# Transposing the codes of x by DMA in place of TensorE in a fused quantized attention-and-LoRA kernel

## The reference

```python
def fake_quant(v, scale, zp):
    q = clip(round(v / scale + zp), 0, 255)
    return (q - zp) * scale

def xattn(x1, x2):                       # for each batch
    return fake_quant(x1, s1, z1) @ fake_quant(x2, s2, z2)

def ffn(x, A, B, Wr):                    # 4 experts of rank 16, top 2
    gates = softmax(keep_top2(x @ Wr.T))
    mid = einsum('tf,erf->ter', x, A)
    return sum_e(gates * einsum('ter,eor->teo', mid, B) * 4)

x = x + tanh(g_xattn) * xattn(layernorm(x), ctx)
x = x + tanh(g_ffn) * ffn(layernorm(x), A, B, Wr)
```

## Time and profile before

| | us |
|---|---|
| time, median of 3 runs | 429.81 (429.75 to 431.95) |
| the profiled execution's own time | 432.26 |
| its span in the profile | 430.5 |
| TensorE busy in the span | 360.3 (84%) |
| VectorE busy | 334.7 (78%) |
| ScalarE busy | 257.6 (60%) |
| GpSimd busy | 85.5 (20%) |
| mean granted clock of TensorE | 0.949 |

### The profile page before, as it was taken

How to read it: one execution, slowest core, us unless ns; L and a number is a source line. 1 busy time by engine, 2 the same in 40 slices (tenths; PEclk the granted TensorE clock), 3 DMA queues, 4 the chain that set the end, 5 groups by cost and what they waited for, 6 DMA issues and landing times. The chain is left out here.

```text
span 430.5 us, 7428 instructions
## 1 busy us (share of the span) xinstructions
PE 360.3 (84%) x2480; PEld 213.2 (50%) x2480; DVE 334.7 (78%) x764; ACT 257.6 (60%) x240; POOL 85.5 (20%) x74
## 2 busy tenths in 40 slices
PE   0063549679989998989899999999999999999954
PEld 0031224265555555555556464756565656565642
DVE  2549994897897979797979787879787878687584
ACT  1655698377859587776767455556464655555140
POOL 1000000130404030222222222222222222224020
PEclk9996779868999999999999999999999999999995
DMA  4999980246755645556472222222222222312022
GB/s 142 344 402 428 424 311 4 97 142 246 251 162 180 190 159 202 185 189 201 150 240 99 99 99 98 99 98 97 97 97 97 97 97 97 99 50 97 2 97 99
DMA packets 22241, 68.52 MB, mean 159 GB/s; under 512 B 3204, under 2 KB 3716, under 8 KB 20100
## 3 DMA queue, kind: packets, MB, share of 16 engines
q1 hardware_dynamic: 22216, 68.20, 44.4%
HBM read 51.42 MB, written 16.78 MB: 158 GB/s over the span
## 5 line engine op out<-in xcount | busy, mean ns | idle before, releaser
L539 PE MATMUL ps_main<-q,q1T 128*128 128x512 f16 x928 | 213.3, 381 | 0.0
L539 PEld LDWEIGHTS ps_main<-q,q1T 128*128 128x128 f16 x928 | 88.1, 99 | 101.9 <-issue 8.5
L404 ACT ACTIVATE h_hi<-x,small_tile 128x1024 f16<-128x1024 f32 x32 | 39.4, 1234 | 65.5 <-DVE small_tile L830 65.5
L349 POOL TENSOR_TENSOR h_lo<-work,h_hi 128x1024 f16<-128x1024 f32 x31 | 66.6, 2148 | 43.7 <-ACT work L409 41.9
L814 DVE SCALAR_TENSOR_TENSOR x<-ps_main,small_tile,xt 128x512 f32<-128x512 f32 x60 | 44.8, 747 | 23.8 <-DMA out_x<-x 14.5
L788 DVE BATCH_NORM_STATS2 small_tile<-xt 128x6 f32<-128x512 f32 x64 | 40.8, 683 | 16.8 <-DMA xt<-in_x 16.7
L343 POOL TENSOR_TENSOR small_tile<-small_tile 128x1 f32<-128x1 f32 x16 | 8.8, 549 | 210.3 <-DVE small_tile L826 210.3
L392 ACT ACTIVATE work<-xt,small_tile 128x1024 uint8<-128x1024 f32 x32 | 38.1, 1234 | 16.0 <-DVE small_tile L804 16.0
L819 DVE BATCH_NORM_STATS2 small_tile<-x 128x6 f32<-128x512 f32 x64 | 44.3, 692 | 1.7
L888 DVE TENSOR_TENSOR x<-ps_delta,x 128x512 f32<-128x512 f32 x64 | 42.3, 683 | 2.7 <-PE ps_delta L605 2.7
L382 ACT ACTIVATE ctx_stage<-ctx_stage,small_tile 128x1024 uint8<-128x1024 f32 x32 | 38.7, 1236 | 5.0 <-DMA ctx_stage<-in_ctx 5.0
(11 more groups left out here) (98 smaller groups left out, 401.9 us busy)
## 6 DMA issues: line engine op xcount, KB each, us to landing
xt<-in_x SPq DMA_DIRECT2D x32, 512.0 KB, 3.7
q<-in_ctx SPq DMA_DIRECT2D x16, 1024.0 KB, 17.8
ctx_stage<-in_ctx SPq DMA_DIRECT2D x32, 512.0 KB, 5.0
out_x<-x SPq DMA_DIRECT2D x64, 256.0 KB, 2.2
x<-in_L_ffn_A SPq DMA_DIRECT2D x1, 512.0 KB
x<-in_L_ffn_B SPq DMA_DIRECT2D x1, 512.0 KB, 15.9
small_tile<-in_L_xattn_x_scale SPq DMA_DIRECT2D x2, 0.5 KB, 4.2
small_tile<-in_L_xattn_x_zp SPq DMA_DIRECT2D x2, 0.5 KB, 4.7
```

Source lines behind the costliest of these rows:

```text
L349: nc.gpsimd.tensor_tensor(h_lo[:, h, :], work[:, h, :], h_hi[:, h, :], ALU.subtract).then_inc(h_lo_ready, 1)
L404: nc.scalar.activation(h_hi[:, h, :], x1[:, b % 2, half(h)], ACT.Identity, bias=h_bias[:, :], scale=h_rstd[:, :]).then_inc(h_hi_ready, 1)
L539: mm = pe.matmul(acc[:, :], q1T[:, b % 2, k, :], q2[:, batch(b), k, cols(n)], start=(k == 0), stop=(k == KT - 1))
```

## The change

From tile 2 on the codes of x are not transposed by TensorE. SP issues two transposing DMAs per tile (`dma_start_transpose`), one for each half of `q1_code`, straight into q1T. They wait for the rounding (x_rounded) and for the products of the tile that last used the buffer (main_done). `turn_q1` and `copy_q1T` are no longer called in the slots; tiles 0 and 1 keep them in the prologue. TensorE's products wait for the DMA's semaphores, and so does ScalarE before it writes `work` again. `turn_hi` waits for the copy of the low part (loT_ready) that last emptied its bank. On SP the two issues stand behind the context load of q = 0 (in slot 1 ahead of it).

```diff
+        q1T_loaded = [sem("q1T_loaded0"), sem("q1T_loaded1")]
...
+            def turn_q1(b, i, h):
+
+                wait(sp, x_rounded, b, i, 2, h + 1)
+                sp.sem_inc(sp_waited, 1)
+                wait(sp, main_done, b, i, NB, -NB)
+                sp.sem_inc(sp_waited, 1)
+                sp.dma_start_transpose(q1T[:, b % 2, h * HK:(h + 1) * HK, :], q1_code[:, h, :]).then_inc(q1T_loaded[h], 16)
+
...
+                if b == 1:
+                    turn_q1(b + 1, i, 0)
+                    turn_q1(b + 1, i, 1)
                 ctx_half(0)
+                if 2 <= b < TILES - 1:
+                    turn_q1(b + 1, i, 0)
+                    turn_q1(b + 1, i, 1)
...
             def normal_half(b, i, h):
-                wait(act, q1_turned, b, i, 2, h + 3)
+                if b == 0:
+                    act.wait_ge(q1_turned, h + 3)
+                else:
+                    wait(act, q1T_loaded[h], b, i, 16, 0)
...
-                    copy_q1T(b + 1, i, 0)
-                    copy_q1T(b + 1, i, 1)
...
-                if ahead:
-                    copy_q1T(b + 1, i, 0)
-                    copy_q1T(b + 1, i, 1)
...
             def turn_q1(b, i, h):
                 wait(pe, x_rounded, b, i, 2, h + 1)
-                wait(pe, loT_ready[h], b, i, 1, -1)
...
                     if n == 0 and k % HK == 0:
-                        wait(pe, q1T_ready, b, i, 2, k // HK + 1)
+                        wait(pe, q1T_loaded[k // HK], b, i, 16, -16)
...
             def turn_hi(b, i, h):
-                if b == TILES - 1:
-                    turn_h(b, i, h, h_hi, h_hi_ready, hi_turned, loT_ready[h], 1, 0)
-                    return
-
-                turn_h(b, i, h, h_hi, h_hi_ready, hi_turned, q1T_ready, 2, 3 + h)
+                turn_h(b, i, h, h_hi, h_hi_ready, hi_turned, loT_ready[h], 1, 0)
...
                         mid_lo(b - 1, i, h)
-                        if b < TILES - 1:
-                            turn_q1(b + 1, i, h)
                     main(b, i, 3, general)
```

More of the change, by code:

```diff
@@ L189, in build @@
         gated_ready, gate_turned, gT_step, gT_ready = sem("gated_ready"), sem("gate_turned"), sem("gT_step"), sem("gT_ready")
-        dve_waited = sem("dve_waited")
+        dve_waited, sp_waited = sem("dve_waited"), sem("sp_waited")
         delta_done, out_ready = sem("delta_done"), sem("out_ready")
@@ L256, in load_x @@
             def load_x(b, i, h):
+                rows = bass.ts(b, P) if isinstance(i, int) else bass.ts(i * 2 + b, P)
                 if b >= 2:
                     wait(sp, x1_ready, b, i, NB, 2 * h + 2 - 2 * NB)
-                rows = bass.ts(b, P) if isinstance(i, int) else bass.ts(i * 2 + b, P)
                 sp.dma_start(xt[:, b % 2, half(h)], x_rows[rows, half(h)]).then_inc(x_loaded[b % 2][h], 16)
@@ L286, in ctx_half @@
                     if b < PER_B - 1:
-                        wait(sp, ctx2_coded, b, i, Q, q + 1)
                         row = (HALVES + Q * (b + 1) + q) // 2
                         rows = bass.ts(row, P) if isinstance(i, int) else bass.ts(i * Q + row, P)
+                        wait(sp, ctx2_coded, b, i, Q, q + 1)
                         load_ctx(rows, q % 2, q)
```

## The result

The change makes no gain; it costs a little. The kernel before took 430.94 us (20 runs, 429.06 to 436.19), the changed one 433.68 us (20 runs, 430.71 to 437.2). The ratio is 1.0058 (95% interval 1.0035 to 1.0082). The prediction of 423.7 us was wrong by 10 us, though the time is inside its range. The profiled execution of after took 433.89 us, with a span of 432.2 us.

A forecast was written before the change was run, and what follows sets the result against it. TensorE's queue was taken to bound the kernel, with a second chain through x almost without slack in late tiles. Gains of 0.45 + 1.4 + 4.2 = 6.1 us off the 429.81 us median gave 423.7 us, range 418 to 441.

The forecast's parts named there:

- The ceiling: TensorE, tiles 2 to 15: sixteen transposes removed per tile, 0.90 us each tile, at most 12.6 us gained.
- the late regime: Slots 8 to 14, TensorE without gaps at 21.1 us per tile: 0.6 us gained per tile, 4.2 us (3.8 to 6.3).
- it fits: Late tiles: the gate's operand would be ready at 301.2, before TensorE reaches it at 301.3, so no new wait.
- The early regime: Slots 2 to 7, while second-batch context is coded: 0.24 us gained per tile, 1.4 us (0 to 4.2).
- The gate's wait of 0.4 us: Early tiles: sign of a right forecast, TensorE's wait for the gate's operand (L594 for L874) grows to 0.4 us.
- Slot 1: First changed slot: only the second eight transposes count, 0.45 us gained (0 to 0.9).
- L: Time from the end of the first rounding until both transposed halves land: taken as 6.9 us, free up to 9.0.
- the two bounds: Landing of one transposing DMA: 2.2 us like a plain one, or 7.7 us like tiny pieces; lower end taken.
- the point of failure: The prediction fails by far if a transposing DMA takes over 5 us, or holds SP so that stores and loads are late.
- Rival 2: Head of each tile: transposing DMA too slow to hide, TensorE stands; 24 us slower, 454 us; chance 0.25.
- What goes from TensorE.: Pricing step: sixteen transposes (L510) leave each of tiles 2 to 15, 0.90 us per tile, 12.6 us at most.
- the rivals: x chain takes gain back, 427.9 us (0.15); slow transposing DMA, 454 us (0.25); full 12.6 us gain, 417.2 us (0.02).

The follow-up runs named there:

- those without a choice: Both kernels with TensorE's branch and the unused program taken out, only the running copy left: kernel before 434.06 us, changed kernel 430.18 us.
- the doubled one: Changed kernel with 136 idle instructions in the unused copy, each transposing DMA issued a second time after the first landed: 480.97 us.
- the second pair: Kernel before and changed kernel, each with TensorE's branch and unused program taken out: 434.06 us and 430.18 us.
- before_shift: Kernel before with the unused copy shortened so the running copy's first wait is instruction 22232, as in the changed kernel: 438.08 us, ratio 1.0145.

## Why the prediction was wrong, by its steps

**The ceiling and the late regime held.** Late slots were to go from 21.1 to 20.5 us and take 20.6 (rows above). Over seven slots, from the weight load of slot 7's gate transpose to that of slot 14, before takes 149.0 us and after 145.8: 3.2 us for 4.2 predicted. Over all profiles but those without a choice and the doubled one, five of the kernel before and six of the changed one, the means are 149.3 and 146.0. The rest of the term is in the timeline of after's slot 10, TensorE and ScalarE:

```profile
300.21 0.99 ACT L440 COPY hT<-ps_turn 128x1024 f16<-128x1024 f16 x1
...
301.26 1.33 PE L593 MATMUL ps_mid<-a_parts,hT 128*128 128x136 bf16 x16 [0.20 <-ACT hT L440]
...
302.42 2.97 PE L551 MATMUL ps_main<-q,q1T 128*128 128x512 f16 x13
...
304.88 0.29 DVE L880 TENSOR_TENSOR gated<-mids,small_tile 128x128 f32<-128x128 f32 x1
...
305.22 0.14 PEld L602 LDWEIGHTS ps_gate<-ident_f,gated 128*128 128x128 f32 x1 [0.33 <-DVE gated L880]
```

The product follows the second half of the low part at once, with no transposes between, as predicted. But the copy L440 (L422 before) now ends last, as the earlier trace rows warned, for 0.20 us, and "it fits" for the gate, with a margin of 0.1, did not hold: its weight load stands for 0.33.

**The early regime is smaller than the pair of profiles says.** Slots 2 to 7 take 136.2 us in before and 134.8 in after, 1.4 less, the very number predicted. The gate's wait of 0.4 us is there:

```profile
197.38 0.33 PE L602 MATMUL ps_gate<-ident_f,gated 128*128 128x128 f32 x1 [0.40 <-DVE gated L880]
```

Yet in the five profiles of the kernel before these slots take 136.2, 137.0, 136.6, 138.1 and 140.4 us, and in the six of the changed one 134.8, 137.9, 138.4, 136.2, 138.3 and 136.3. The means are 137.7 and 137.0. These slots scatter by more than the term, and three of the six carry the wait at tile 2. Part of the scatter is the clock: 140.4, 137.9 and 138.3 each hold one slot of 23.9 to 25.4 us in which the granted clock falls behind a wait of some 1.7 us (0.93 in the mean of the slot). Without these three the means are 137.0 and 136.4. So the pair doesn't show a gain of 1.4, and that it met the number is luck; slot 2's wait is a cost that the prediction did not have.

**Slot 1** was to gain 0.45 and lost 0.4 in the pair; both are inside that scatter.

**The DMAs.** L was taken as 6.9 us and may be up to 9.0. In slot 10 the first rounding ends at 299.96 (299.21 plus 0.75), the DMAs are issued from 300.14, and the second lands near 305: L is about 5, under even the lower of the two bounds. The view of line 291 in after (duration of the issue in ns, then the landing):

```profile
L291 SPq DMA_TRANSPOSE q1T<-work x28: 1231/1246/4000, 100.4 to 384.7; - x28
...
DMA to landing us min/median/max: 3.1/3.8/8.3
```

The Trainium skill's 1309 ns for a 128x128 block ("VectorE: DVE Perf Modes", "The three transpose paths") is no pace: a DMA of 8 such blocks lands in 3.1 us at best, where that pace gives an estimated 10.5. Nor does it land in the 1 us that the prediction estimated from a bandwidth. In the early slots single ones take up to 6.6 us, over the 5 us that the prediction named as the point of failure, and TensorE waits for none of them in this profile. Rival 2 is out for the late slots. One wait at tile 2 is all that came of it in the early ones.

**The step that failed** is the first: "What goes from TensorE." I priced 224 transposes by their time in the slots and did not count that their code goes twice, once from the copy that runs and once from the copy that doesn't, and that this moves the target of a jump that costs 7.6 us in the trace of before. That row, the branch L698 with 7577 ns, was there to be read, and so was the idle time of 22.26 us "<-issue" ahead of the first L510. I read the table of stretches from slot 1 on and took the opening as unchanged because its instructions are unchanged. What no row of before told is that the new target would be the one of the five places tried that brings the gap; that is bad luck. The sum in its own terms: predicted 6.1, and at equal start 3.6 to 4.4 (430.94 less 427.33, 434.06 less 430.18, 431.04 less 426.90, 438.08 less 433.68). Only the second pair was timed side by side; by the ratios to the kernel before, each timed beside its own kernel, the four pairs give 3.7 to 5.4 us. Then 7 us are put back by the gap. The chance of 0.25 for slower was for another mechanism, rival 2; none of the rivals was this, and that the time lies inside the range is luck.

## What to carry to other kernels

Read the opening of the trace, down to the sequencer's branches, even where the diff does not touch it: with a far jump ahead of the work, an edit that changes the number of instructions can move the start by 7 us either way. Before you judge a small change on a kernel with such a jump, compare the first instruction of each engine in both profiles, or pad the unused copy and time it at two places. Putting the copy that runs next to the branch takes the far jump out of the opening. Here it made neither kernel faster than a start without the gap (430.94 us in both orders, and 427.33 against 426.90), and no run shows whether the jump at the end can meet the same gap.

## What was not expected of the hardware

- A jump over some 22,000 instructions of TensorE takes 5.9 to 6.4 us (7.6 in one execution) at the opening, and 90 ns where the target is next to it.
- Behind a jump, one instruction more in code that never runs takes away a second stall of 6.3 to 7.1 us. It was seen at the same instruction number (22232) in two different kernels, and not at 22233, 22234, 22368 or 22512.
- In five of the profiles, besides that of the doubled DMAs, the granted clock falls once or twice in the early slots, each time behind a wait of TensorE of 1.70 to 1.75 us (0.50 from 240 to 243 us in `before_shift`, where slot 7 takes 25.4 us). The wait alone doesn't decide it: in the same profile slots 4 to 6 have waits of 1.71 to 1.74 us and keep the full clock.
- A transposing DMA of 256 KB holds SP's queue for 1.25 us, against 0.35 us for a plain load of x, and for up to 4.0 us in slot 1, behind five other loads. It lands in 3.1 to 8.3 us; the packets under 512 bytes went from 3,204 in the kernel before to 32,772.
- An earlier start is not always a shorter time: the kernel before starts at 17.2 us with its copies turned round and at 19.9 as it is, and takes 430.9 us both times. The lead is gone by slot 7; why is open.
